# Graph attention on one core: the gathers of the wide rows in twos, their softmax in later batches

## What is computed

```python
def reference(x, adj, L0_gnn_W, L0_gnn_a):
    h = jnp.maximum(_layernorm(x, axis=-1), 0.0)
    h = h @ W
    s_src = h @ a_src
    s_dst = h @ a_dst
    e = jax.nn.leaky_relu(s_src[:, None] + s_dst[None, :], negative_slope=0.2)
    e = jnp.where(adj > 0, e, jnp.float32(-9000000000000000.0))
    attention = jax.nn.softmax(e, axis=1)
    return x + attention @ h
```

## Time and profile before

| | |
|---|---|
| median of 3 runs | 804.93 us (803.57 to 805.2) |
| span of the profiled execution | 858.3 us |
| VectorE busy | 592.4 us (69%) |
| ScalarE busy | 525.0 us (61%) |
| GpSimd busy | 512.0 us (60%) |
| TensorE busy | 445.4 us (52%) |
| moved by DMA | 299.31 MB |
| mean granted TensorE clock | 0.721 |

### The profile page before, as it was taken

How to read it: one execution, slowest core, us unless ns; L and a number is a source line. 1 busy time by engine, 2 the same in 40 slices (tenths; PEclk the granted TensorE clock), 3 DMA queues, 4 the chain that set the end, 5 groups by cost and what they waited for, 6 DMA issues and landing times.

```text
span 858.3 us, 8941 instructions
## 1 busy us (share of the span) xinstructions
PE 445.4 (52%) x1823; PEld 213.9 (25%) x1855; DVE 592.4 (69%) x3125; ACT 525.0 (61%) x371; POOL 512.0 (60%) x522
## 2 busy tenths in 40 slices
PE   4787555555555546545554545475055567533421
PEld 3652222222222222212122222132022222211221
DVE  7956577777777767566678767767177788755784
ACT  3979777666767667766387777666154877732000
POOL 3745666666656665765655666667636665665571
PEclk9888678677676777766677777777578767765555
DMA  8999999999999999989599999999659799992110
GB/s 339 424 370 419 404 408 408 408 411 407 410 409 409 408 409 405 399 315 393 217 415 411 408 409 408 408 401 409 233 210 394 277 408 409 411 402 92 25 38 11
DMA packets 40903, 299.31 MB, mean 349 GB/s; under 512 B 11052, under 2 KB 14034, under 8 KB 24464
## 3 DMA queue, kind: packets, MB, share of 16 engines
q1 hardware_dynamic: 22976, 276.83, 79.3%
q0 software_dynamic: 15328, 17.58, 6.6%
q10 hardware_dynamic: 2544, 4.33, 1.5%
HBM read 304.31 MB, written 8.65 MB: 365 GB/s over the span
## 4 chain that ended last, share of the span: by engine, by line
DVE 72%; another core or an unknown queue 11%; issue 8%; PE 5%; ACT 2%; DMA 0%; POOLq 0%; DVEq 0%; ACTq 0%
DVE x_all L821 18%; DVE rest L638 5%; DVE words L636 5%; DVE words L640 4%; PE banks L1049 3%; DVE wf L666 2%; DVE top L680 2%; DVE top_bit L662 2%; DVE cand L676 2%; DVE cand L723 1%; DVE one_hot L768 1%; DVE e L785 1%; DVE top_bit L672 1%; DVE top L727 1%
## 5 line engine op out<-in xcount | busy, mean ns | idle before, releaser
L361 POOL DMA_INDIRECT gathered<-table,index x448 | 448.7, 1002 | 295.1 <-DVE index L714 151.4
L467 ACT ACTIVATE mask_buf<-adj_buf,minus_half 128x2048 bf16<-128x2048 int32 x252 | 489.5, 1992 | 141.3 <-issue 56.5
L1049 PE MATMUL banks<-mask_buf,bit_ident 128*128 128x512 bf16 x992 | 316.6, 472 | 37.6 <-issue 24.7
L821 DVE SCALAR_TENSOR_TENSOR x_all<-gathered,weight,x_all 128x128 f32<-128x128 f32 x512 | 157.5, 348 | 16.1 <-DVE x_all L821 7.6
L1049 PEld LDWEIGHTS banks<-mask_buf,bit_ident 128*128 128x128 bf16 x1024 | 113.2, 121 | 203.4 <-issue 137.6
L1061 PE MATMUL banks<-is_wide,before 128*128 128x1 bf16 x64 | 6.9, 176 | 207.9 <-DVE is_wide L751 155.9
L1090 PE MATMUL banks<-x_all,one_hot 128*128 128x128 f32 x128 | 35.4, 368 | 74.1 <-DVE x_all L821 39.0
L481 ACT ACTIVATE prob<-e 128x16 f32<-128x16 f32 x31 | 6.5, 208 | 103.6 <-issue 72.7
L636 DVE MAX8 words<-banks 128x8 f32<-128x512 f32 x64 | 44.3, 693 | 25.4 <-PE banks L1049 18.7
L1061 PEld LDWEIGHTS banks<-is_wide,before 128*128 128x128 bf16 x64 | 4.5, 112 | 227.8 <-DVE is_wide L751 170.8
L640 DVE MAX8 words<-rest 128x8 f32<-128x512 f32 x64 | 44.5, 695 | 2.4 <-DVE rest L638 0.2
(11 more groups left out here) (162 smaller groups left out, 589.4 us busy)
## 6 DMA issues: line engine op xcount, KB each, us to landing
adj_buf<-in_adj SPq DMA_DIRECT2D x128, 2048.0 KB
gathered<-table,index POOLq DMA_INDIRECT x448
table<-gathered ACTq DMA_DIRECT2D x4, 1040.0 KB, 14.0
x_all<-in_x SPq DMA_DIRECT2D x3, 1024.0 KB, 10.8
out<-x_all SPq DMA_DIRECT2D x2, 1280.0 KB
x_all<-in_x SPq DMA_DIRECT2D x2, 512.0 KB, 5.1
out<-x_all SPq DMA_DIRECT2D x1, 1024.0 KB
w_gathered<-table,w_index POOLq DMA_INDIRECT x24
```

Of the source, the lines that this page charges most:

```text
L361: nc.gpsimd.indirect_dma_start(g_cols[buf][:, k, :], None, table, bass.IndirectOffsetOnAxis(index[:, buf, k:k + 1], 0), bounds_check=N, oo ...
L467: nc.scalar.activation(mask_buf[:, u], adj_buf[:, u], ACT.Sign, bias=minus_half[:]).then_inc(mask_ready, 1)
L821: ins = v.scalar_tensor_tensor(at[b], g_view[par][b][:, k, 0:F], weight[:, b, k:k + 1], at[b], ALU.mult, ALU.add)
L1049: ins = mm(bank, bit_ident[:, h * PART_BITS + c], mask_buf[:, u, c * BIT_COLS:(c + 1) * BIT_COLS], start=False, stop=(h == PARTS - 1 and c ...
```

## The change

Four lags and a run length become constants. The wide gathers are issued `WIDE_RUN` = 2 at a time behind the gathers of batches end+3 to end+7 (the fifth time only the gather from `x` is left); the wide logits move from the end of batch end+6 to that of end+8, and the wide sum from end+7 to end+10. The wide exponential moves from the middle of batch end+7 to the start of batch end+10 on ScalarE. The third group's steps stay where they are.

```diff
--- before.py
+++ after.py
@@ -22,6 +22,11 @@
 COUNT_LAG = 1
 RECORD_LAG = 2
 SUMS_LAG = 4
+WIDE_INDEX_LAG = 2
+WIDE_GATHER_LAG = 3
+WIDE_LOGITS_LAG = 8
+WIDE_SUM_LAG = 10
+WIDE_RUN = 2
 GROUP_ENDS = (9, 19, 31)
 GROUPS = len(GROUP_ENDS)
 GROUP_STARTS = (0, 10, 20)
@@ -381,15 +386,16 @@
                     pool.wait_ge(index_ready, indexed(i))
                     gather(buf, 0, COLUMNS, gathers_done[buf])
 
-            def wide_gather(g):
+            def wide_gather(g, lo=0, hi=MORE + 1):
                 pool.wait_ge(w_index_ready, g + 1)
-                for k in range(MORE):
+                for k in range(lo, min(hi, MORE)):
                     nc.gpsimd.indirect_dma_start(
                         w_gathered[:, k, :], None, table, bass.IndirectOffsetOnAxis(w_index[:, g, k:k + 1], 0),
                         bounds_check=N, oob_is_err=False).then_inc(w_gathers, 16)
-                nc.gpsimd.indirect_dma_start(
-                    w_x[:, g, :], None, x, bass.IndirectOffsetOnAxis(w_index[:, g, MORE:MORE + 1], 0),
-                    bounds_check=N - 1, oob_is_err=False).then_inc(w_gathers, 16)
+                if hi > MORE:
+                    nc.gpsimd.indirect_dma_start(
+                        w_x[:, g, :], None, x, bass.IndirectOffsetOnAxis(w_index[:, g, MORE:MORE + 1], 0),
+                        bounds_check=N - 1, oob_is_err=False).then_inc(w_gathers, 16)
 
             def wide_store(g):
 
@@ -402,8 +408,9 @@
             for i in range(BATCHES):
                 gather_batch(i)
                 for g in range(GROUPS - 1):
-                    if i == GROUP_ENDS[g] + 3:
-                        wide_gather(g)
+                    lo = (i - GROUP_ENDS[g] - WIDE_GATHER_LAG) * WIDE_RUN
+                    if 0 <= lo <= MORE:
+                        wide_gather(g, lo, lo + WIDE_RUN)
             wide_gather(GROUPS - 1)
             for g in range(GROUPS):
                 wide_store(g)
@@ -490,13 +497,13 @@
 
             act.wait_ge(mask_ready, FIRST_DONE)
             for i in range(BATCHES):
+                for g in range(GROUPS - 1):
+                    if i == GROUP_ENDS[g] + WIDE_SUM_LAG:
+                        wide_softmax(g)
                 for u in range(FIRST_DONE if i == 0 else 0, UNITS):
                     mask(i, u)
                     if u == 2 and i >= SUM_LAG:
                         softmax(i - SUM_LAG)
-                    for g in range(GROUPS - 1):
-                        if u == 5 and i == GROUP_ENDS[g] + 7:
-                            wide_softmax(g)
                     if u == 6 and i == LAST:
                         softmax(LAST - 2)
             softmax(LAST - 1)
@@ -894,11 +901,11 @@
 
             def wide_steps(i):
                 for g in range(GROUPS - 1):
-                    if i == GROUP_ENDS[g] + 2:
+                    if i == GROUP_ENDS[g] + WIDE_INDEX_LAG:
                         wide_index(g)
-                    if i == GROUP_ENDS[g] + 6:
+                    if i == GROUP_ENDS[g] + WIDE_LOGITS_LAG:
                         wide_logits(g)
-                    if i == GROUP_ENDS[g] + 7:
+                    if i == GROUP_ENDS[g] + WIDE_SUM_LAG:
                         wide_sum(g)
 
             for i in range(LAST):
```

## The result

| | before | after |
|---|---|---|
| median | 805.2 us (803.57 to 807.7, 9 runs) | 809.1 us (806.54 to 809.26, 9 runs) |
| ratio to before | | 1.0032, 95% interval 1.0017 to 1.0048 |

The account below looks back on a forecast made before the run. The prediction took the adjacency-matrix loads to bound the kernel. The parts summed to 6.6 + 14.8 = 21.4 us in the profiled execution, but the floor left 1.4 us, so it took 0.6 us: 804.3 us, range 795 to 809.

Parts of the forecast that it names:

- What bounds the kernel: Whole kernel: adjacency loads nearest to full at 400 to 411 GB/s, broken behind the ends of wide groups 0 and 1.
- The 34 and 40 us batches: Batches 13 and 23, behind the two group ends: 34.09 and 40.74 us against 22.46 undisturbed.
- VectorE's crawl: Batch 13's decoding: VectorE slowed while GpSimd issued nine wide gathers, one microsecond for one, 11.6 us too many.
- the 14.07 us wait: Batch 16: ScalarE waits for the wide logits before the wide exponential, later masks queued behind; expected to fall to 8.5 us.
- the floor by 409 GB/s: Whole kernel: 732 us for 299.31 MB plus 71.6 us of tail, 803.5 us, 1.4 us under the median.
- Part 1, the gathers: Spreading GpSimd's wide gathers behind groups 0 and 1: gain between nothing and 6.6 us in the profiled execution.
- Part 2, logits and exponential: Later wide logits, exponential and sum at both groups: at most 14.8 us of empty DMA time gained in the profiled execution.
- the forecast case: Plain run: both orders hidden, no measurable change, 804.3 us, own range 803.3 to 806.5; chance 0.46.
- Part 3, what stays: Third group and tail: untouched, tail keeps its 83.3 us, reuse adds no new wait; cost 0, at most 3.3 us.
- (a): Groups 0 and 1: starvation real in plain runs; whole 791.0 us, chance 0.11; a third 800.3 us, chance 0.25.
- (b): Batches with 16 gathers: 2.8 us longer each, some 2 us paid per group, 809 us; chance 0.18.
- The signs to watch: Profile after: no 34 or 40 us batch, DMA shares above 0.95, span 10 to 20 us shorter, plain time within 2 us.

Follow-up runs that it names:

- b_again: The kernel before, unedited, measured and profiled a second time; ratio 0.9992 (0.9981 to 1.0003), span 800.7 us.
- block_late: The changed kernel with WIDE_RUN = 9, so nine gathers in one block and the later logits, exponential and sum kept; ratio 0.9997 to the kernel before.
- run5: The changed kernel with WIDE_RUN = 5: five gathers behind batch end+3, four behind end+4, late logits; ratio 1.0008 to the kernel before.
- extra28: The kernel before with two extra gathers, into a tile nobody reads, behind each of batches 12 to 25; ratio 1.0103.
- spread_g0: The changed kernel with only group 0's gathers in twos, group 1's in one block, late logits; ratio 0.9998 to the kernel before.
- extra5: The kernel before with five extra gathers, into a tile nobody reads, behind batch 25; ratio 1.0046.

## Why the prediction was wrong

**What bounds the kernel.** Wrong in what it read from the trace. The 34 and 40 us batches, VectorE's crawl and the 14.07 us wait were one execution's. The text did doubt them for a plain run, and that doubt was right: the floor by 409 GB/s left 1.4 us of room for the groups, and `b_again` shows that they cost nothing. That the floor came so close to the median was luck, though. The stretch of 545 us in `b_again` ran at 399 GB/s, not 409 (750 us for the bytes, not 732), and from its last mask to the end are 52.9 us at a share of 0.11 (47 us to add, not 71.6): two errors of some 20 us that nearly cancel.

The Trainium skill gives about 436 GB/s as the ceiling of the DMA side (SBUF — State Buffer, the section on the two sides of the memory). The trace doesn't reach it: batch 7 of the changed kernel has 408 GB/s at a share of 1.01, and the stretch of 545 us has 399 at 1.00.

**Part 1, the gathers.** Right that nine moved gathers are hidden in the batches either way. The reading that VectorE crawls one microsecond for each of GpSimd's was of the disturbed execution only. Right that lateness of 11.7 us or 2.6 us reaches no reader: batch 13 has 22.48 us before and 22.62 after.

**Part 2, logits and exponential.** 0, as the forecast case had it; `block_late` shows it alone. The 14.8 us were never in the kernel.

**Part 3, what stays.** This is the step that failed. The prediction says: "The third group is untouched (a block of nine behind the last batch), so the tail of 83.3 us keeps its length." Its instructions are the same, its length is not. GpSimd's closing drain grew from 6.84 to 9.37 us, by 2.53 us, nearly all of the 2.6 us that the ratio gives; the stretch from the last mask to the end grew from 52.9 to 55.5 us. The term was costed at nothing because its instructions keep their places, without a look at what the tail's last instruction is. Such a look would have shown a drain of 6.84 us, but not that its length depends on where gathers stood in much earlier batches. The 83.3 us themselves were inflated by the disturbed execution: 57.1 us of them lie behind the start of its last mask, for 52.9 in `b_again`.

**The rivals.** (a), a gain, is refuted by `block_late` and `b_again`. (b) gave the sign and, by luck, the size: 809 us stood there for batches too full of gathers. Its mechanism is refuted by `run5`, with 19 gathers in a batch and no later loads, and by `extra28` at 0.3 to 0.5 us per batch. The slower side held 0.18 of the chances, and the measured 809.1 lies just over the range's end.

**The signs to watch.** Of those named for the profile after, shares above 0.95 came true, and so did batches near 22.5 us: batches 13 to 16 take 22.45 to 22.84 us, and 17 takes 24.18, but so does batch 7 with 24.08, far from any wide gather. The span shrank by 52 us, more than the 10 to 20 named, and the text was right that this would say nothing of the time. One sign misled: a rise was to mean that "20.8 us of gathers do not fit a batch". The time rose, and they do fit.

## What to carry to other kernels

When the span of a profiled execution and the median of the runs are some per cent apart, profile once more before pricing any wait in it. A transfer moved in the middle can lengthen the last instruction (here by 2.53 us): compare the engines' closing drains, and where an engine waits anyway near the end, put a drain there. When the loads set the pace, as here at a DMA share of 1.00, a change that only moves other engines' work about has nothing to gain in the batches, whatever their waits look like.

## What was not expected of the hardware

GpSimd's closing drain lasts 6.84 to 10.52 us here and depends on where in its sequence earlier indirect transfers stood, though the total of 478 is the same; gathers added behind batches 27 to 29 lengthen it by 0.082 us each. Three orders of the gathers (that of the kernel before and `block_late`, `run5`, `spread_g0`) share 6.84. Taken as steps of 0.082, the drains of 7.99, 9.37, 10.27 and 10.52 us lie 14, 31, 42 and 45 transfers above 6.84, and a batch has 14. `extra5`, with five more gathers behind batch 25, lies 32 above. That looks like a count of transfers since some clearing event; it is an estimate from these lengths alone. What the event is was not tried and stays open.
